# Tile counting of a graph layer: five units of 328 tiles, dealt out between the gathered groups

## The chip, the cores and the metric

The kernel runs on one core of one Trainium2 chip. The time is the device time of one execution in microseconds, here 2799.81 us as the median of three runs.

## The reference

A node-feature table `x` (12,500 nodes by 256) goes through a layer norm, a graph layer, a second layer norm and a mixture of eight experts. The graph layer is what the change touches:

```python
def _L0_gnn_ref(node_feats, src, dst, eps, W1, b1, W2, b2, gamma, beta):
    neigh = jax.ops.segment_sum(node_feats[src], dst, num_segments=n)
    h = (1.0 + eps) * node_feats + neigh
    h = jax.nn.relu(h @ W1 + b1) @ W2 + b2
    mean = jnp.mean(h, axis=0)
    var = jnp.mean(jnp.square(h - mean), axis=0)
    h = (h - mean) * jax.lax.rsqrt(var + BN_EPS) * gamma + beta
```

There are 200,000 edges, sorted by destination: `dst = int(12500 * u**2)` for random `u`, so the first nodes have by far the most edges. The sources are random.

## The kernel before

The 200,000 edges are 1563 tiles of 128 edges, in the order of their destinations. `stage_edges` sums the source rows of every edge into the destination rows in two ways, and mixes both.

**Gathered groups.** A group is 8 tiles (GT). GpSimd issues one indirect DMA per tile (L744), which brings 128 source rows of the node table into a buffer; there are three buffers (RG), and three groups make an iteration. GpSimd may refill a buffer when TensorE has released it (`s_free`, at the end of `gathered`, L795). VectorE makes the one-hot matrices of the group's destinations (L1005 `e_rel`, L1010 `e_hot`), TensorE multiplies them with the gathered rows (L790, 16 matmuls), and VectorE adds the sums of the group before into the node blocks (L993, two instructions). A group whose destinations lie in two blocks does this once per block (a window). A register word per group says which blocks.

**Counted tiles.** The hottest 256 tiles (HT) are not gathered. VectorE makes two one-hot matrices of a tile (L1046 and L1048: source block by destination column, and source row), TensorE multiplies them into a tally in PSUM (L808), and VectorE adds the tally into the matrix `counts` (98 source blocks by 136 columns) at the column of the destination (L1063). Four tiles in a row share a tally at first, then two, then one (g in SEGMENTS), as long as they span at most five destinations (TW). When the tiles of a unit are counted, VectorE folds the last eight columns (L1098), TensorE multiplies `counts` with the whole node table, which SyncE brings in 25 pieces of 512 KB (L704, L830), VectorE adds the product to two node blocks (`spread`, L1075), and ScalarE clears `counts` for the next unit (L904, 13 instructions). There are three units (SEGMENTS), of 144, 64 and 48 tiles.

**The order.** Each engine runs its own program, and the order in each is fixed by the same list of iterations. `sections` walks over them: `build` iterations first count 24 or 16 tiles, in bodies of eight, and then handle the three gathered groups; four `mix` iterations (MIX) handle two pieces behind each group; `plain` iterations are groups alone, with a quad at the end of most.

**Quads.** A quad is 512 nodes, whose edges are all in. It goes through the two layers on TensorE (L840 transposes, L848, L854) and ScalarE (L912, L915, L920), and its statistics on VectorE (`measure`, L1085; the copy for the transposes is L1090). `AT` says behind which iteration a quad stands; quads 1 to 24 follow one another from iteration 27 on, quad 0 stands behind iteration 25, and the last quad behind everything.

A test on the edge list in `stage_norm` decides whether the counting fits the data; if not, a general and slow path takes all edges (`general_rounds`).

What a group waits for on VectorE and TensorE stands in these lines:

```python
                        dve.wait_ge(s_sum, turn)
                        dve.wait_ge(s_add, turn)
                        add_window(dve.snap(1 - place)).then_inc(s_add, 1)
```

## Time and profile before

| | |
|---|---|
| median of 3 runs | 2799.81 us (2795.89 to 2807.99) |
| profiled execution | 2807.59 us |
| its span | 2805.5 us |
| mean granted TensorE clock | 0.808 |
| TensorE matmuls busy | 1710.0 us (61%) |
| VectorE busy | 1451.2 us (52%) |
| ScalarE busy | 674.4 us (24%) |
| GpSimd busy | 1805.8 us (64%) |
| gathers (L744) | 1320, 955 ns on average |
| HBM read, written | 275.92 MB, 75.58 MB |

The span is measured from the first to the last instruction of the program, the execution's time lies 2.1 us above it. GpSimd is the busiest engine, but no engine is near 100%: the program has four stages with different limits (norms and table until about 130 us, edges until about 1957 us, routing until about 2190 us, experts until the end). The change is in the second stage. A busy share over the whole span says little about it; what counts is which engine sets its pace and what that engine waits for.

### The profile page before, as it was taken

How to read it: one execution, taken by the hardware profiler on the slowest of the kernel's cores; microseconds unless marked ns; L12 is line 12 of the kernel's file. 1: busy time of each engine (PE TensorE's matmuls, PEld its weight loads, DVE VectorE, ACT ScalarE, POOL GpSimd, SP SyncE). 2: the span in 40 equal slices, each digit the busy share in tenths (PEclk: the TensorE clock that was granted, in tenths of full speed). 3: DMA queues.
4: the chain of work that ended last, by engine and by line, in shares of the span. 5: the costliest groups of instructions: out<-in, count | busy, mean ns of one | idle time of the engine just before them, and what ended most of it. 6: DMA issues, size and time to landing. Idle time of an engine off the chain costs nothing. (4 is left out here: it accounts for less than half of the span.)

```text
span 2805.5 us, 39125 instructions
## 1 busy us (share of the span) xinstructions
PE 1710.0 (61%) x9059; PEld 1019.1 (36%) x9060; DVE 1451.2 (52%) x4196; ACT 674.4 (24%) x1061; POOL 1805.8 (64%) x1798
## 2 busy tenths in 40 slices
PE   0045555446445566777745665577664888979984
PEld 0012222113212233333323333344553555656663
DVE  8856642573265222323323322332786566858885
ACT  6610000000000001111100110012664654535543
POOL 0066667667757767777777777771355577857876
PEclk9986567567757678999968878798665899989997
DMA  7533357336725744433333333332663322140220
GB/s 237 194 96 106 99 168 235 103 108 200 227 86 156 230 143 121 128 113 105 105 106 106 106 106 105 105 104 38 202 215 127 99 79 81 33 141 24 86 92 15
DMA packets 201051, 345.76 MB, mean 123 GB/s; under 512 B 65494, under 2 KB 129324, under 8 KB 200871
## 3 DMA queue, kind: packets, MB, share of 16 engines
q0 software_dynamic: 74304, 195.51, 24.0%
q1 hardware_dynamic: 124422, 146.96, 16.4%
q8 instruction: 93, 1.52, 0.2%
q10 hardware_dynamic: 2144, 1.05, 0.1%
q14 instruction: 88, 0.71, 0.1%
HBM read 275.92 MB, written 75.58 MB: 125 GB/s over the span
## 5 line engine op out<-in xcount | busy, mean ns | idle before, releaser
L744 POOL DMA_INDIRECT e_got<-table,e_idx x1320 | 1260.6, 955 | 514.2 <-issue 383.5
L790 PE MATMUL e_sums<-e_got,e_hot 128*128 128x256 f16 x2720 | 463.1, 344 | 509.3 <-DMA e_got<-table,e_idx 341.6
L790 PEld LDWEIGHTS e_sums<-e_got,e_hot 128*128 x2720 | 316.7, 121 | 666.8 <-issue 580.1
L993 DVE SCALAR_TENSOR_TENSOR nodes<-e_sums,above,nodes x171 | 82.6, 483 | 705.8 <-PE e_sums L790 690.8
L1665 POOL TENSOR_TENSOR x_midl<-x_midf,x_midh 128x512 f16<-128x512 f32 x200 | 293.9, 1497 | 96.6 <-ACT x_midh L1784 92.3
L808 PE MATMUL e_tally<-w2f 128*128 128x490 f16 x256 | 124.4, 542 | 302.1 <-DVE w2f L1048 298.8
L1010 DVE TENSOR_SCALAR e_hot<-ring,e_rel x1360 | 249.1, 275 | 65.2 <-DVE e_rel L1005 59.5
L1741 PE MATMUL x_down<-x_w2h,x_midh 128*128 128x256 f16 x736 | 203.9, 277 | 14.3 <-DVE x_yb L1884 12.5
L912 ACT ACTIVATE e_hT<-e_up 128x1024 f32<-128x1024 f32 (+1 forms) x25 | 25.2, 1006 | 746.6 <-PE e_up L840 746.6
L1741 PE MATMUL x_down<-x_w2l,x_midh 128*128 128x256 f16 x736 | 204.0, 277 | 0.0
L1741 PE MATMUL x_down<-x_w2h,x_midl 128*128 128x256 f16 x736 | 203.8, 277 | 0.0
L1680 POOL DMA_INDIRECT out<-x_res,x_nodei x128 | 141.9, 1108 | 88.7 <-DVE x_res L1899 51.3
L848 PE MATMUL e_up<-e_hT,W1s 128*128 128x512 f32 (+1 forms) x400 | 179.1, 602 | 27.4 <-ACT e_hT L912 27.4
L854 PE MATMUL e_up<-e_mid,W2s 128*128 128x512 f32 (+1 forms) x400 | 174.9, 590 | 19.2 <-ACT e_mid L915 19.2
L808 PEld LDWEIGHTS e_tally<-w2f 128*128 128x128 f16 x256 | 26.3, 103 | 397.3 <-issue 396.9
L904 ACT ACTIVATE counts<-e_zero 128x536 f32<-128x536 f32 (+1 forms) x39 | 20.6, 615 | 611.8 <-PE e_product L830 611.8
L1270 POOL DMA_INDIRECT slot_rows<-r_row,r_slots x100 | 97.5, 975 | 98.3 <-DVE r_slots L1496 74.5
L1717 PE MATMUL x_up<-x_xTh,x_w1h 128*128 128x512 f16 (+1 forms) x400 | 148.7, 372 | 3.2 <-ACT x_midh L1784 3.2
L1717 PE MATMUL x_up<-x_xTl,x_w1h 128*128 128x512 f16 (+1 forms) x400 | 148.1, 370 | 0.0
L1717 PE MATMUL x_up<-x_xTh,x_w1l 128*128 128x512 f16 (+1 forms) x400 | 148.1, 370 | 0.0
L1784 ACT ACTIVATE x_midf<-x_up,x_b1s 128x512 f32<-128x512 f32 x200 | 138.6, 693 | 23.8 <-PE x_up L1717 13.8
L1784 ACT ACTIVATE x_midh<-x_up,x_b1s 128x512 f16<-128x512 f32 x200 | 137.5, 688 | 0.0
(209 smaller groups left out, 2681.9 us busy)
## 6 DMA issues: line engine op xcount, KB each, us to landing
w1f<-table SPq DMA_DIRECT2D x72, 512.0 KB, 4.5
e_got<-table,e_idx POOLq DMA_INDIRECT x1320
slot_rows<-e_zero SPq DMA_DIRECT2D x64, 268.0 KB, 2.7
x_row<-slot_rows SPq DMA_DIRECT2D x32, 536.0 KB, 7.3
table<-n_pair SPq DMA_DIRECT2D x25, 512.0 KB, 3.0
counts<-in_x SPq DMA_DIRECT2D x24, 512.0 KB, 5.0
r_xin<-in_x SPq DMA_DIRECT2D x24, 512.0 KB, 5.0
out<-r_row SPq DMA_DIRECT2D x24, 512.0 KB, 3.3
```

The source lines that it names most:

```text
L744: pool.indirect_dma_start(got[:, r, t, :], None, table.rearrange("p h d -> (p h) d"), bass.IndirectOffsetOnAxis(ap=idx[:, r, t:t + 1], axi ...
L790: ins = nc.tensor.matmul(sums[:, place, 0:D], hot[:, place, t, :], got[:, r, t, half * D:(half + 1) * D], start=(t == 0 and half == 0), st ...
L808: nc.tensor.matmul(tally[:, i // g % 2, 0:KEY], tall[:, i % OR, KEY:OH], tall[:, i % OR, 0:KEY], start=(i % g == 0), stop=(i % g == g - 1) ...
L848: ins = nc.tensor.matmul(up[:, c % 2, 0:width], W1s[:, j, c * P:(c + 1) * P], hT[:, j, 0:width], start=(j == 0), stop=(j == DK - 1))
L854: ins = nc.tensor.matmul(up[:, c, 0:width], W2s[:, j, c * P:(c + 1) * P], mid[:, j, 0:width], start=(j == 0), stop=(j == H1C - 1))
L1010: ins = nc.vector.tensor_scalar(hot[:, place, t, :], plan.ring[:, ring_at(shift)], rel[:, place, t:t + 1], None, ALU.is_equal)
L1270: pool.indirect_dma_start(buf, bass.IndirectOffsetOnAxis(ap=slots[:, j, t:t + 1], axis=0), row[:, j, t, :], None, bounds_check=bound, oob_ ...
L1665: nc.gpsimd.tensor_tensor(midl[:, j % 2, c, :], midf[:, c % MB, :], midh[:, j % 2, c, :], ALU.subtract).then_inc(s_mlo, 1)
L1680: pool.indirect_dma_start(out, bass.IndirectOffsetOnAxis(ap=nodei[:, j, t:t + 1], axis=0), res[:, r, t, :], None, bounds_check=bound, oob_ ...
L1717: ins = nc.tensor.matmul(up[:, c % MB, 0:tiles * P], w[:, h, k, cols], x[:, j % 2, k, 0:tiles * P], start=(n == 0), stop=(n == len(passes) ...
L1741: ins = nc.tensor.matmul(down[:, t, :], m[:, j % 2, k, rows], w[:, h, k, :], start=(n == 0), stop=(n == len(passes) - 1))
L1784: ins = nc.scalar.activation(m, up[:, c % MB, :], ACT.Relu, bias=b1s[:, h, c:c + 1], scale=MID_SCALE / (X_SCALE * W_SCALE))
```

## The change

The tiles to be counted are now 328, in five units of 144, 64, 48, 40 and 32 tiles. `UNIT_TILES` lists how many tiles an iteration has: 24 in the first four, 16 in the next three, 8 in all others that count. They are dealt out over the three groups of the iteration (`tiles_at`): 24 as 8, 8, 8; 16 as 5, 5, 6; 8 as 2, 3, 3, each share ahead of its group. Tiles up to 96 share a tally by four, up to 168 by two, the rest have one each. The gathered groups are 155 instead of 165 (NG), in 52 iterations instead of 55.

VectorE adds a group's tally one group late: after the one-hots of the next tile, also across a gathered group (`counted`); before, each body of eight ended with the last tally's add. The column of each add is loaded by itself; before, one load brought the columns of a body.

Units and quads now overlap: `AT` gives every quad an iteration and a place in it, from iteration 10 on. Eleven quads stand in iterations that count tiles, nine in mixed ones, and four in the last two iterations, where quads 0, 22, 1 and 23 stand at (50, 0), (50, 2), (51, 0) and (51, 2). `spread` stands in the iteration behind the last piece, and ScalarE's clearing behind the quads of the last mixed iteration. All loops over iterations in this stage but GpSimd's are written out; so are the loops of SyncE in `stage_norm` and of GpSimd's scatter in routing. The constants:

```diff
-SEGMENTS = (((4, 24, 4), (2, 24, 2)), ((1, 16, 2), (3, 16, 1)), ((3, 16, 1),))
-NU = len(SEGMENTS)
-BODY = 8
+UNIT_TILES = ((24, 24, 24, 24, 16, 16, 16), (8,) * 8, (8,) * 6, (8,) * 5, (8,) * 4)
+GROUPS = ((96, 4), (168, 2), (328, 1))
+NU = len(UNIT_TILES)
...
-NIT = -(-(ET - HT) // (GT * RG))
-NG = NIT * RG
+NG = -(-(ET - HT) // GT)
+NIT = -(-NG // RG)
...
+SPREAD = {n + 1: u for n, (u, i) in MIXED.items() if i == MIX - 1}
+AT = {2: (10, 2), 3: (13, 2), 4: (16, 2), 5: (18, 2), 6: (22, 2), 7: (24, 2), 8: (26, 2), 9: (28, 2), 10: (31, 2),
+      11: (33, 2), 12: (34, 2), 13: (36, 2), 14: (38, 2), 15: (40, 2), 16: (41, 2), 17: (43, 2), 18: (44, 2),
+      19: (46, 2), 20: (47, 2), 21: (49, 2), 0: (50, 0), 22: (50, 2), 1: (51, 0), 23: (51, 2)}
...
+        def tiles_at(n, r):
+
+            tiles = TILES.get(n, ())
+            return tiles[len(tiles) * r // RG:len(tiles) * (r + 1) // RG]
```

On TensorE:

```diff
-                def build(u, start, n, first, tiles, g):
-
-                    if u > 0:
-                        pe.wait_ge(s_clear, u)
-                    with pe.Fori(start, start + n) as it:
-                        with pe.Fori(0, tiles // BODY):
-                            for i in range(BODY):
-                                pe.wait_ge(s_tall, tile)
-                                pe.reg_add(tile, tile, 1)
-                                nc.tensor.matmul(tally[:, i // g % 2, 0:KEY], tall[:, i % OR, KEY:OH], tall[:, i % OR, 0:KEY],
-                                                 start=(i % g == 0), stop=(i % g == g - 1)).then_inc(s_tile, 1)
-                        for r in range(RG):
-                            gathered(it, r)
...
+                for n in range(NIT):
                     for r in range(RG):
-                        gathered(n, r)
...
+                        for t in tiles_at(n, r):
+                            count(t)
+                        if n * RG + r < NG:
+                            gathered(n, r)
+                        for number in pieces_at(n, r):
+                            piece(number)
+                        for q in quads_at(n, r):
+                            quad(q)
                 quad(NQ - 1, LAST)
```

On ScalarE:

```diff
+                blank(0)
+                for n in range(NIT):
+                    if n in SPREAD and SPREAD[n] + 1 < NU:
+                        blank(SPREAD[n] + 1)
+                    for r in range(RG):
+                        for q in quads_at(n, r):
+                            quad(q)
```

On VectorE:

```diff
-                            for i in range(BODY):
-                                one_hots(i)
-                                if i % g == 0 and i > 0:
-                                    count(i // g - 1, g)
-                            count(BODY // g - 1, 0)
...
+                def count(group):
+
+                    last_tile = len(GROUP_OF) - 1 - GROUP_OF[::-1].index(group)
+                    column = dve.value_load(plan.cols[0:1, group:group + 1], min_val=0, max_val=P - 1)
+                    dve.wait_ge(s_tile, OR + last_tile + 1)
+                    if group > 0:
+                        dve.wait_ge(s_count, group)
...
+                def counted(t):
+
+                    one_hots(t)
+                    if t in FIRST:
+                        dve.wait_ge(s_blank, (FIRST.index(t) + 1) * COUNT_ZEROS)
+                    elif GROUP_OF[t - 1] != GROUP_OF[t]:
+                        count(GROUP_OF[t - 1])
...
+                        for t in tiles_at(n, r):
+                            counted(t)
+                        if n * RG + r < NG:
+                            gathered(n, r)
+                        if n in SPREAD and r == 0:
+                            spread(SPREAD[n])
+                        for q in quads_at(n, r):
+                            quad(q)
```

**TensorE, from the end of a quad to the next gathered group.** Before, in the loop of plain iterations (L848 and L854 are the quad's layers, L790 the group's matmuls; ISA rows work on registers):

```order
L854 MATMUL e_up<-e_mid,W2s 128x512 [waits e_mid_s]
L854 MATMUL e_up<-e_mid,W2s 128x512 x7
L873 REGISTER_ALU
L873 COMPARE_AND_BRANCH
L779 TENSOR_LOAD words
L779 ISA x2
L782 ISA [waits e_got0]
L783 UNCONDITIONAL_BRANCH
L787 ISA [waits e_add,e_hot_s]
```

Now, behind iteration 13:

```order
L831 MATMUL e_up<-e_mid,W2s 128x512 [waits e_mid_s]
L831 MATMUL e_up<-e_mid,W2s 128x512 x7
L796 MATMUL e_tally<-w2f 128x490 [waits e_tall_s] x2
L774 TENSOR_LOAD words
L774 ISA x2
L777 ISA [waits e_got0]
L778 UNCONDITIONAL_BRANCH
L782 ISA [waits e_add,e_hot_s]
```

Two tallies of the next iteration now stand between the quad and the group.

**VectorE, the tiles in front of a group's one-hots.** Before, one of the eight tiles of a body in a unit counted one by one (L1046 and L1048 make the one-hots, L1063 adds the tally before):

```order
L1053 ISA [waits e_tile]
L1046 TENSOR_SCALAR w2f<-iota,key 128x490
L1053 ISA
L1048 TENSOR_SCALAR w2f<-iota,low 128x128
L1050 ISA
L1060 ISA [waits e_count,e_tile]
L1063 TENSOR_TENSOR counts<-counts,e_tally 128x98x5
L1065 REGISTER_ALU
```

Now, from the copy of a quad's rows (L1027) to the first one-hots of the next iteration's first group:

```order
L1027 TENSOR_SCALAR e_hT<-nodes 128x1024
L975 TENSOR_SCALAR w2f<-iota,key 128x490 [waits e_tile]
L977 TENSOR_SCALAR w2f<-iota,low 128x128
L983 TENSOR_LOAD cols
L983 ISA x2
L988 ISA [waits e_count,e_tile]
L988 TENSOR_TENSOR counts<-counts,e_tally 128x98x5
...
L947 TENSOR_LOAD words
L947 ISA x2
L951 UNCONDITIONAL_BRANCH
L951 ISA
L953 REGISTER_ALU
L953 TENSOR_SCALAR e_rel<-cold,least,base 128x8
```

The six rows from L975 to L988 stand twice, where the line of dots is, and the group's `e_rel` and one-hots come behind the second add. Each add has a load of its own.

## Rows read from the trace of the kernel before

**Rows 1.** The line of the gather: durations (min, median, max) in ns, then idle time before it.

```profile
L744 POOL DMA_INDIRECT e_got<-table,e_idx x1320: 940/946/4984, 136.6 to 1904.5; - x189
...
  PEq L795: 123.9, 57
```

**Rows 2.** Timeline at the stage's end: start us, us, engine, line, names.

```profile
1904.52 0.95 POOL L744 DMA_INDIRECT e_got<-table,e_idx  x1 [0.30 <-issue]
...
1957.45 1.52 DVE L1372 BATCH_NORM_AGGREGATE r_bnv<-stats 128x2 f32<-128x150 f32 x2 [0.30 <-PEq L663]
```

**Rows 3.** Timelines of GpSimd and TensorE, 170 to 192 us, first counting iterations.

```profile
169.94 1.04 POOL L744 DMA_INDIRECT e_got<-table,e_idx  x1 [0.30 <-issue]
180.25 0.94 POOL L744 DMA_INDIRECT e_got<-table,e_idx  x1 [9.27 <-PEq L795]
...
175.71 3.59 PE L790 MATMUL e_sums<-e_got,e_hot 128*128 128x256 f16 x16 [4.02 <-DVE e_hot L1010]
...
186.34 1.92 PE L790 MATMUL e_sums<-e_got,e_hot 128*128 128x256 f16 x16 [1.72 <-DVE nodes L993]
189.14 0.99 PE L808 MATMUL e_tally<-w2f 128*128 128x490 f16 x4 [0.88 <-DVE w2f L1048]
```

**Rows 4.** Timelines of GpSimd, TensorE and ScalarE around quad 1, 1041 to 1090 us.

```profile
1042.44 0.95 POOL L744 DMA_INDIRECT e_got<-table,e_idx  x1 [0.30 <-issue]
...
1054.65 3.59 PE L790 MATMUL e_sums<-e_got,e_hot 128*128 128x256 f16 x16 [6.38 <-DMA e_got<-table,e_idx]
1064.95 3.59 PE L790 MATMUL e_sums<-e_got,e_hot 128*128 128x256 f16 x16 [6.70 <-DMA e_got<-table,e_idx]
...
1079.05 7.13 PE L854 MATMUL e_up<-e_mid,W2s 128*128 128x512 f32 x16 [0.78 <-ACT e_mid L915]
1086.02 1.91 PE L790 MATMUL e_sums<-e_got,e_hot 128*128 128x256 f16 x16
1089.64 1.92 PE L790 MATMUL e_sums<-e_got,e_hot 128*128 128x256 f16 x16 [1.71 <-DVE nodes L993]
...
1086.32 1.26 ACT L920 ACTIVATE nodes<-e_up,b2s 128x512 f32 x2 [7.32 <-PE e_up L854]
```

**Rows 5.** Windows: stretch, length, busy PE, PEld, DVE, ACT, POOL, granted clock, DMA share, GB/s.

```profile
150.00:390.00 240.00, 123.97 (x456) 52.19 (x456) 158.70 (x566) 0.55 (x2) 148.90 (x155) 0.68 0.35 106
390.00:500.00 110.00, 63.83 (x266) 32.20 (x266) 24.74 (x101) 0.00 (x0) 83.19 (x89) 0.72 0.68 224
1300.00:1400.00 100.00, 72.01 (x296) 39.73 (x296) 33.40 (x128) 15.11 (x21) 75.71 (x80) 0.93 0.37 105
```

**Rows 6.** Timelines of GpSimd and TensorE in mixed iteration 7, 397 to 424 us.

```profile
398.12 0.95 POOL L744 DMA_INDIRECT e_got<-table,e_idx  x1 [0.30 <-issue]
...
412.43 3.59 PE L790 MATMUL e_sums<-e_got,e_hot 128*128 128x256 f16 x16 [4.80 <-DMA e_got<-table,e_idx]
```

**Rows 7.** Timelines of VectorE: a tally's latency at 157 us, single tiles at 577 us.

```profile
157.51 0.67 DVE L1063 TENSOR_TENSOR counts<-counts,e_tally 128x490 f32 x1 [0.85 <-PE e_tally L808]
...
577.12 0.33 DVE L1046 TENSOR_SCALAR w2f<-iota,key 128x490 f16<-128x490 f16 x1
...
577.53 0.66 DVE L1063 TENSOR_TENSOR counts<-counts,e_tally 128x490 f32 x1
578.10 0.49 DVE L1046 TENSOR_SCALAR w2f<-iota,key 128x490 f16<-128x490 f16 x1
```

**Rows 8.** Timelines of VectorE: gathered groups at 560 us, a second window at 1885 us.

```profile
560.48 0.29 DVE L1005 TENSOR_SCALAR e_rel<-cold,least,base  x1 [0.72 <-issue]
561.12 1.43 DVE L1010 TENSOR_SCALAR e_hot<-ring,e_rel  x8 [0.35 <-DVE e_rel L1005]
...
564.65 0.29 DVE L1005 TENSOR_SCALAR e_rel<-cold,least,base  x1 [0.97 <-issue]
...
1885.18 0.30 DVE L1005 TENSOR_SCALAR e_rel<-cold,least,base 128x8 f32 x1 [0.29 <-issue]
```

**Rows 9.** Groups of instructions, 136 to 1906 us: the piece matmuls.

```profile
L830 PE MATMUL e_product<-w1f,counts 128*128 128x512 f16 x294 | 89.2, 452 | 19.5 <-DMA w1f<-table 14.4
```

**Rows 10.** Timeline of ScalarE, 490 to 520 us: the clearing of the counts.

```profile
500.15 6.87 ACT L904 ACTIVATE counts<-e_zero 128x536 f32<-128x536 f32 x13 [349.60 <-PE e_product L830]
```

More of the change, by code:

```diff
@@ L325, in _ @@
                     load(q, q, 0)
-                with sp.Fori(1, NQ // R5 - 1) as it:
+                for it in range(1, NQ // R5 - 1):
                     for j in range(R5):
@@ L813, in mix, with count @@
[L813 to L827 removed]
+                def count(t):
+                    group = GROUP_OF[t]
+                    pe.wait_ge(s_tall, t + 1)
+                    nc.tensor.matmul(tally[:, group % 2, 0:KEY], tall[:, t % OR, KEY:OH], tall[:, t % OR, 0:KEY],
+                                     start=(t == GROUP_OF.index(group)), stop=(group not in GROUP_OF[t + 1:])
+                                     ).then_inc(s_tile, 1)
@@ L832, in piece, with quad @@
                     ins.then_inc(s_used, 1)
-                def quad(k, width=QN):
-                    if not (isinstance(k, int) and k == 0):
+                def quad(q, width=QN):
+                    k = ORDER.index(q)
+                    if k > 0:
                         pe.wait_ge(s_h2, k * DK)
@@ L1129, in _, with quad @@
-                tile = counter(dve, "tile", 1)
-                counted = counter(dve, "counted", 1)
-                columns = [dve.alloc_register(f"column{i}") for i in range(BODY)]
-                dve.sem_inc(s_count, 1)
-                sections(build, mix, plain)
+                        nc.vector.bn_stats(stats[:, c, q * 6:q * 6 + 6], nodes[:, q, c * QN:c * QN + width])
+                def quad(q):
+                    k = ORDER.index(q)
+                    if k > 0:
+                        measure(ORDER[k - 1])
+                    nc.vector.tensor_scalar(hrow.rearrange("p t d -> p (t d)"), nodes[:, q, :], 1.0, None,
+                                            ALU.mult).then_inc(s_hrow, 1)
@@ L1274, in _ @@
                 pool.wait_ge(s_rows, 1)
-                walk(pool, [(scatter, 0)], NQ, R5)
+                for q in range(NQ):
+                    scatter(q, q % R5)
                 for j in range(R5):
```

303 lines of the change are left out of this document (94 added, 209 removed).

## The prediction

> **What bounds the kernel now.** I read four views in this order: the gather's own line, the timeline around its waits, the timeline of a counting iteration and of a quad, and the windows for the granted clock. The change lies in the stage that gathers edges, from the first gather at 136.6 us to the start of the next stage at 1957.5 us [rows 1, 2]. GpSimd issues its 1320 gathers. One takes 0.95 us and the next starts 1.25 us after it [rows 1, 3]: 1320 x 1.2515 = 1652 us of a stretch of 1904.5 + 1.0 - 136.6 = 1769 us. The missing 117 us are waits: 57 waits for TensorE's release (L795), 123.9 us with the usual 0.3 us in each [rows 1], 6.8 us for late index lists, and 4.0 us of one long first gather (4984 ns). So 112.5 us are real waits, 93% of the stretch is GpSimd's own pace, and only two things can shorten it: fewer gathers, or fewer waits. A group is 8 gathers, 10.0 us; an iteration three groups, 30.0 us.
>
> Where do the waits come from? From the iterations that count tiles. At 169.94 + 1.04 GpSimd stops; 24 tiles must be counted first, then TensorE multiplies the group at 175.71 for 3.59 us, and 0.95 us after its end GpSimd goes on, 9.27 us late [rows 3].
>
> **How late TensorE may be.** A group whose first gather started at 1042.44 is multiplied from 1054.65, 12.2 us later [rows 4]. Its buffer is wanted 3 x 10.0 us after that start, 0.95 us after the release [rows 3]. With 3.6 us of matmuls the slack is 30.0 - 0.95 - 12.2 - 3.6 = 13.3 us. A quad (the node blocks' two layers) sits between two groups on TensorE: matmuls of one group end at 1064.95 + 3.59 = 1068.54, those of the next at 1086.02 + 1.91 = 1087.93 [rows 4]. That is 19.4 us for one group, 9.4 over the pace, and below 13.3: in the old plain loop a quad costs nothing. This works because VectorE had the next one-hots ready while TensorE was in the quad.
>
> **Fewer gathers.** 165 groups become 155: 80 gathers x 1.2515 = **-100.2 us**, on the bounding engine. The 72 tiles that replace them cost no gather. The two new units read the table twice more (50 pieces of 512 KB); in the old mixed iterations the gathers kept their pace with the pieces beside them, and the DMA share was 0.68 [rows 5], so I book nothing for them. Their price is a later landing: a mixed group that began at 398.12 was multiplied from 412.43, after 14.3 us instead of 12.2 [rows 6, 4]. Between 0 and 2.1 us I take 1.3 off the slack there, nearer that row.
>
> **The old waits.** Tiles dealt out 8, 5 or 2 to 3 before each group no longer make 24 stand in a row: **-112.5 us** if nothing took their place.
>
> **What takes their place.** New is that 11 quads share iterations with tiles. The one-hots of a group now stand on VectorE behind the counts of its tiles, and with one tile per count each count waits for a tally that TensorE can make only after the quad. So from the end of a quad: tally and its latency 0.6 (0.85 from the end of the tile's one-hots, which are ready here [rows 7]), count 0.6 [rows 7], load of the group's word, `rel` and one-hots 0.97 + 0.29 + 0.35 + 1.43 = 3.0 [rows 8], 0.3 to the matmul, 1.9 us of it. Release to release: 17.6 + 6.4 = 24.0, and about 1 us because VectorE copies the quad's rows only after its adds: **15 us over the pace**, more than 13.3. Where the group after the quad has no tile it stays 10.3.
>
> How fast is that won back? A group costs VectorE 564.65 - 560.48 = 4.17 us [rows 8]; a tile with its count 578.10 - 577.12 = 0.98 us, some a little more, so 1.04 [rows 7]. With 2.67 tiles that is 6.95 us, and a load of the column in front of each count comes on top. That load isn't visible alone. Bounds: nothing (it runs behind the one-hots, 0.25 us of them), or the 0.68 us by which a group's first `rel` (0.97 us of idle) comes later than one without the load and two branches (0.29 us) [rows 8]; I take 0.25, nearer the lower end since one-hots run ahead of it. So 7.6 us with TensorE at its upper level (2.4 GHz). At its lower (1.2), the chain is 0.3 + 3.59 + 0.9 [rows 3] + 0.6 to the first count, 0.6 + 1.1 for the next, 3.0: 10.1 us. In the old counting iterations both matmul lengths stand side by side (3.59 and 1.92; see 1.92 right behind a quad [rows 3, 4]) at a granted clock of 0.68, while 1300 to 1400, with quads, had 0.93 [rows 5]. The middle is 8.8: **1.2 us won back per group**.
>
> The Trainium skill ("DMA: Bandwidth & Descriptors", Latency and other measured facts) puts the floor of a `tensor_load` at about 600 ns. The rows' 0.68 us, with two branches in it, agrees. If all 220 counts paid it openly it would be 132 us on VectorE, and the sum would be that of the slower rival below.
>
> A quad that finds the slack used up by the last one waits 15 less what the groups in between (its own excluded) won back. By iteration: 13: 0.6 (8 groups, whose tiles are partly counted in pairs, so 1.8 each); 16: 15 - 8 x 1.2 = 5.4; 18: 10.3 - 6 = 4.3; 24 and 26: 15 - 5 x 1.2 = 9 each; 28: 4.3; 33: 8.1 (the boundary behind 32, below, left 4.5 of slack); 34, right behind it: 15 - 2 x 1.2 = 12.6; 36: 9; 43: 9; 44: 12.6. Sum **+84**.
>
> **The unit boundaries.** Behind iterations 10, 22 and 41 a quad is followed by ScalarE's clearing of the counts: ten last piece matmuls at 0.30 [rows 9] make 3, quad 17.6, ScalarE's last copies end 1.4 later (1087.58 against 1086.18 [rows 4]), clearing 6.9 [rows 10], tile, count and one-hots 5.3, matmuls 3.6 = 38, or 28 over. Less 13.3, and 1.3 for the landing: 16 each, and 7 more at 41, where a quad at 40 had used up slack. Sum **+55**. Before, ScalarE's clearing was followed by a stall too, but of 24 or 16 tiles. Behind 32 there is no quad: 3 + 6.9 + 5.3 + 3.6 = 18.8, 8.8 over, no wait. **Unit 0** has no quads; 8 tiles in fours cost 4.17 + 8 x 0.41 + 2 x 0.82 = 9.1 us a group on VectorE, some 10.5 at the low level; 12 groups by 0.5: **+6**.
>
> **The end.** Iterations 46 to 51 hold 7 quads and the last short one. On TensorE: 7 x 17.6 + 17.6, 21 windows (a group's one-hots and matmuls run once per window; the last groups have two) x 3.62 (1089.64 - 1086.02 [rows 4]), 98 piece matmuls x 0.30 [rows 9] = 246, plus 12.2 to the first: 258, with a copy here and there 260 us. The old 17 last groups took 170 and another 52 from the last gather to the stage's end [rows 2], 222. **+38**. TensorE is what is late there, not the gathers.
>
> Unrolled loops in the first stage and in routing: nothing; GpSimd and SyncE wait for data there.
>
> **Sum.** -100.2 - 112.5 + 84 + 55 + 6 + 38 = **-30 us**. The profiled execution took 2807.6 us (span 2805.5), so 2778; against the median of the runs shown (2799.8) the same step gives **2770 us**.
>
> **Rivals.**
> 1. *Slower: nothing is won back in counting iterations.* Place: VectorE's count in front of a group's one-hots. It decides once a group with tiles takes 10 us or more, that is with TensorE at the lower level (10.1 us above) or loads in the open. Then the eleven quads cost about 145, boundaries 58, unit 0 20, the end 45: 268, against 212.7 gained: **+55, 2855 us**. For: 0.68 of granted clock where tiles were counted, and every matmul after a pause ran 3.59 us. Against: quads now lie between, and with quads it was 0.93. Chance 0.30.
> 2. *Faster: TensorE stays at the upper level and the load hides.* Won back 2.4 per group: quads 38, boundaries 47, end 38: 123. **-90, 2710 us**. Chance 0.15.
> 3. *The counting never holds up one-hots*, all waits go, only the end is dearer: -212.7 + 38 = **-175, 2625 us**. Against it: the order of the program, tallies behind the quad. Chance 0.03.
> 4. *The change doesn't do what it says*: the program tests the edge list and falls back to a slow general path if a count's tiles span more than 5 destinations, or a unit more than 128. From the reference's formula the widest group spans 5 exactly, the units 105 to 116; the last counted destination is 548 of 1024 allowed. It should hold. Otherwise hundreds of us slower. Chance 0.02.
>
> **How the numbers follow.** Forecast 0.50. Its own spread (load 0 to 0.68, 0.6 to 1.8 us won back) is -75 to +20. A measurement of this kernel can tell about 0.5% (14 us) from no change. Of the forecast's 0.50, 0.29 lie below -14, 0.17 within, 0.04 above; of rival 1's 0.30, 0.03 lie within. Faster: 0.29 + 0.15 + 0.03 = 0.47. Same: 0.20. Slower: 0.04 + 0.27 + 0.02 = 0.33. The range takes in rivals 1 and 2: 2705 to 2860; outside lie rivals 3 and 4 and the tails, under 0.2. The forecast's own range is 2725 to 2820.
>
> **What would show it.** 1240 gathers; GpSimd's waits for L774's release about 150 us, at iterations 11, 23 and 42 (14 to 22 us each), and after 24, 26, 33, 34, 36, 43 and 44 (9 to 13); hardly any in iterations 0 to 10. After a quad, the tally at once and the group's matmuls 4 to 5 us later instead of at once. A count's idle before it of 0 to 0.5 us. From the last gather to the next stage 70 to 80 us instead of 52. The forecast is wrong if groups with tiles that follow a quad come at more than 9.5 us (rival 1) or at under 8 (rival 2), or if the waits at 11, 23 and 42 are missing.

## The result: 7827 us, and the profile after

| | before | changed |
|---|---|---|
| median of the runs, us | 2798.5 (4 runs, 2795.9 to 2808.0) | 7826.8 (4 runs, 7819.4 to 7831.8) |
| ratio | | 2.795, 95% interval 2.788 to 2.802 |
| span of the profiled execution, us | 2805.5 | 7829.9 |
| granted clock, mean | | 0.934 |
| instructions recorded | | 65731 |

The forecast was 2770 us. The changed kernel takes 5028 us more than the old one, and no wait of a GpSimd-bound stage could be that large: the page has to be read for work that was not there before. Lines of the page of the changed kernel, its first line and four groups of instructions (columns: line, engine, operation, out<-in, count, busy and mean ns of one, idle before them and what ended it):

```profile
span 7829.9 us, 65731 instructions
...
L719 POOL DMA_INDIRECT e_got<-table,e_some x1568 | 1485.3, 947 | 3584.6 <-DMA e_some<-targets 3163.3
L760 PE MATMUL e_sums<-e_got,e_hot 128*128 128x256 f16 x3904 | 909.9, 413 | 4296.2 <-DMA e_got<-table,e_some 3957.8
...
L728 POOL DMA_INDIRECT e_got<-table,e_idx x1240 | 1179.5, 951 | 539.5 <-issue 366.4
...
L912 DVE SCALAR_TENSOR_TENSOR nodes<-e_sums,nodes 128x256 f32 x488 | 207.2, 425 | 3476.5 <-PE e_sums L760 3476.5
```

The line of the gather [rows 1] has become two. L728, with 1240 gathers of 951 ns, is what the prediction described. L719 is another place in the program: the general path, that handles all edges four tiles at a time with indices loaded into `e_some`. 1568 gathers are 392 rounds of 4, all edges of the list. GpSimd is idle for 3163 us of them, waiting for the next round's lists. The timeline of GpSimd in the changed kernel shows one round and the change-over (columns: start, length, engine, line, names, idle before):

```profile
136.52 4.32 POOL L719 DMA_INDIRECT e_got<-table,e_some  x1 [6.38 <-DMA e_some<-targets]
...
152.97 0.94 POOL L719 DMA_INDIRECT e_got<-table,e_some  x1 [8.37 <-DMA e_some<-targets]
154.22 0.95 POOL L719 DMA_INDIRECT e_got<-table,e_some  x1 [0.30 <-issue]
...
5199.12 0.95 POOL L719 DMA_INDIRECT e_got<-table,e_some  x1 [0.30 <-issue]
5207.57 0.95 POOL L728 DMA_INDIRECT e_got<-table,e_idx  x1 [7.50 <-PEq L768]
```

From 136.5 to 5207.6 us, 5071 us, the slow path runs, 12.9 us a round; nothing overlaps, since one round's lists, gathers, matmuls and adds follow each other. In the middle of that stretch VectorE starts one round's add at 2512.51, SyncE asks for the next lists at 2512.53, the gathers run from 2515.37 to 2520.06, the matmuls start at 2522.32 and the next add at 2524.44. Then the stage of the prediction runs as well, from 5207.6 to the next stage at 6990.3 us: 1783 us, where before it took 1821 [rows 2]. It adds nothing there: with `general` set the program gives it destinations and keys of -1, which match no row, and one window for every group (2480 matmuls at L785, 2560 in the repaired kernel below). So the 1783 us don't measure the change.

So the fourth rival had come about, "the change doesn't do what it says". The program itself decides: VectorE computes a list of conditions on the sorted destinations, and `general` is the number of rounds of the slow path, 0 if all hold. The list has six conditions (`wrong[0]` to `wrong[5]`), and the prediction had examined three: the span of a count, the width of a unit, the last counted destination. Two of the others ask for the order of the counted tiles; by the reference's formula both hold. The sixth is `wrong[3]`, fed by `BOUNDS` and `closed_before`:

```
return max([0] + [QN * (q + 1) for q, (it, _) in AT.items() if it <= group // RG])
...
then(nc.vector.tensor_tensor(wrong[3], block8[:, 0, :], bound, ALU.add))
```

A quad overwrites the rows of 512 nodes; from its iteration on, no group may still bring an edge to one of them. The table puts quad 5 (nodes 2560 to 3071) behind iteration 18. By the reference's formula the first group of iteration 18, group 54, starts at destination 2970, 102 too low. Every other quad of the table satisfies the condition, the closest quad 9 with 5 to spare (the old table's closest, quad 23, had 40). That was arithmetic; the runs had to show it.

### The profile page after: what moved, and what is told of

It is laid out like the page before. It is cut to its first block and busy times, and to the rows that moved or that the text cites. A ratio compares the mean times of both kernels' runs of the same rounds, so it can differ in the third digit from the quotient of the medians.

```text
span 7829.9 us, 65731 instructions
## 1 busy us (share of the span) xinstructions
PE 2688.4 (34%) x12991; PEld 1538.8 (20%) x12992; DVE 2252.5 (29%) x7571; ACT 688.4 (9%) x1087; POOL 3209.3 (41%) x3284
## 5 line engine op out<-in xcount | busy, mean ns | idle before, releaser
L719 POOL DMA_INDIRECT e_got<-table,e_some x1568 | 1485.3, 947 | 3584.6 <-DMA e_some<-targets 3163.3
L760 PE MATMUL e_sums<-e_got,e_hot 128*128 128x256 f16 x3904 | 909.9, 413 | 4296.2 <-DMA e_got<-table,e_some 3957.8
L760 PEld LDWEIGHTS e_sums<-e_got,e_hot 128*128 128x128 f16 x3904 | 501.8, 137 | 4703.6 <-issue 4515.4
L728 POOL DMA_INDIRECT e_got<-table,e_idx x1240 | 1179.5, 951 | 539.5 <-issue 366.4
L912 DVE SCALAR_TENSOR_TENSOR nodes<-e_sums,nodes 128x256 f32 x488 | 207.2, 425 | 3476.5 <-PE e_sums L760 3476.5
L785 PE MATMUL e_sums<-e_got,e_hot 128*128 128x256 f16 x2480 | 486.8, 380 | 402.9 <-DVE e_hot L958 243.5
L870 ACT ACTIVATE e_hT<-e_up 128x1024 f32<-128x1024 f32 (+1 forms) x25 | 25.2, 1007 | 6358.6 <-PE e_up L817 6312.9
L785 PEld LDWEIGHTS e_sums<-e_got,e_hot 128*128 x2480 | 318.6, 133 | 577.0 <-issue 467.2
L906 DVE TENSOR_SCALAR e_hot<-iota,e_rel 128x128 f16<-128x128 f16 x1952 | 376.7, 256 | 17.4
L920 DVE CAST e_somef<-e_some 128x4 f32<-128x4 int32 x392 | 66.6, 170 | 670.5 <-DMA e_some<-targets 664.3
L958 DVE TENSOR_SCALAR e_hot<-ring,e_rel x1240 | 229.6, 274 | 59.8 <-DVE e_rel L953 55.3
L988 DVE TENSOR_TENSOR counts<-counts,e_tally 128x490 f32 x220 | 146.4, 666 | 302.4 <-PE e_tally L796 270.3
L1649 PE MATMUL x_down<-x_w2h,x_midh 128*128 128x256 f16 x736 | 203.0, 276 | 14.5 <-DVE x_yb L1792 12.6
L975 DVE TENSOR_SCALAR w2f<-iota,key 128x490 f16<-128x490 f16 x328 | 120.6, 368 | 150.7 <-ACT counts L865 132.7
```

Source lines behind the costliest of these rows:

```text
L719: pool.indirect_dma_start(got[:, 0, t, :], None, table.rearrange("p h d -> (p h) d"), bass.IndirectOffsetOnAxis(ap=some[:, 0, t:t + 1], ax ...
L728: pool.indirect_dma_start(got[:, r, t, :], None, table.rearrange("p h d -> (p h) d"), bass.IndirectOffsetOnAxis(ap=idx[:, r, t:t + 1], axi ...
L760: ins = nc.tensor.matmul(sums[:, 0, 0:D], hot[:, 0, t, :], got[:, 0, t, half * D:(half + 1) * D], start=(t == 0 and half == 0), stop=(t == ...
L785: ins = nc.tensor.matmul(sums[:, place, 0:D], hot[:, place, t, :], got[:, r, t, half * D:(half + 1) * D], start=(t == 0 and half == 0), st ...
L906: ins = nc.vector.tensor_scalar(hot[:, place, t, :], plan.iota[:, 0:P], rel[:, place, t:t + 1], None, ALU.is_equal)
L912: return nc.vector.scalar_tensor_tensor(out=row, in0=sums[:, place, 0:D], scalar=1.0 / X_SCALE, in1=row, op0=ALU.mult, op1=ALU.add)
```

## The experiments

Ratios are to the kernel before, run beside the new one on the same chip.

**1. One number: quad 5 one iteration later.**

```
-AT = {2: (10, 2), 3: (13, 2), 4: (16, 2), 5: (18, 2), ...
+AT = {2: (10, 2), 3: (13, 2), 4: (16, 2), 5: (19, 2), ...
```

> One number differs from the changed kernel: quad 5 (nodes 2560 to 3071) stands behind iteration 19 instead of 18. Theory A, found after the result: the changed kernel's own list, not its work, fails the test that a quad may only close once all groups with its edges are past (group 54, the first of iteration 18, starts at destination 2970, 102 below 3072), and so the 392 rounds of the slow path ran. Then here the 1568 gathers of that path are gone, 1240 are left, and the time falls by about 5000 us, to 2770 us by the sum of the prediction (2710 to 2855 with its neighbours), with waits of 14 to 22 us at iterations 11, 23 and 42. Rival B: another condition fails too (spans of a count, a unit's width). Then the slow path still runs and the time stays at 7827 us. Rival C: the new order is slow by itself, and the slow path is only part of the 5000 us: over 3000 us remain.

Measured: 2773.9 us (4 runs, 2771.1 to 2782.0), ratio 0.988 (0.986 to 0.991). The slow path is gone, 5053 us with it. Theory A of the expectation holds; its rivals B (another condition fails too) and C (the new order is slow by itself) fall. The forecast for a kernel that does what it says was 2770.

**2. The slow path forced in the kernel before.** The condition for quad 23 made stricter by 64.

```
-    return max([0] + [QN * (q + 1) for q, it in AT.items() if it <= group // RG])
+    return max([0] + [QN * (q + 1) + (64 if q == NQ - 2 else 0) for q, it in AT.items() if it <= group // RG])
```

> The kernel before, with the condition for quad 23 made stricter by 64 destinations, which its list does not meet (its margin there is 40); nothing else is changed, and its order of work is the old one. Theory A (the slow path is an addition of its own, whatever order follows): 392 rounds of 13 us come in front, about +5050 us, so 7850 us, 24 to 25 us off the changed kernel's 7827 plus or minus what the new order is worth by itself. Rival C (part of the 5000 us belongs to the new order): clearly less, under 7000 us.

Measured: 7932.4 us (2 runs), ratio 2.827. Groups of instructions of GpSimd in that run:

```profile
L732 POOL DMA_INDIRECT e_got<-table,e_some x1576 | 1501.3, 953 | 3652.2 <-DMA e_some<-targets 3220.4 <-issue 431.9
L744 POOL DMA_INDIRECT e_got<-table,e_idx x1320 | 1257.4, 953 | 499.9 <-issue 384.8 <-PEq L795 107.2 <-PEq L773 7.5
```

394 rounds cost 5127 us over the 2805.6 of the kernel before, 13.0 us a round, against 12.9 in the changed kernel. The slow path costs the same in either; the new order is not slow. The expected 7850 took 5050 us for 392 rounds, 12.9 each; two more rounds and 0.1 us each make up most of the difference. An order that leaves quad 5 at 18 and drops the test was not tried: it would read the quad's rows before the last edges are added to them.

From here on the repaired kernel is what the prediction's sum is held against, and the other runs change one thing in it.

**3. Tiles counted behind their group instead of ahead.** In the loops of TensorE and VectorE the loop over `tiles_at(n, r)` stands behind `gathered(n, r)`.

> As the first run, but the tiles dealt to a group are counted behind it instead of ahead of it, on TensorE and on VectorE. By the prediction's step on quads: the next group's one-hots are then ready during a quad, so a quad costs 19.4 us from group to group again instead of 24 to 25, and the +84 us for eleven quads among tiles falls to about 0 to 20; the boundaries stay. So 60 to 80 us below the first run of this call, about 2695 us. Rival: the order behind or ahead does not matter, since the next group's one-hots wait for its tally anyway once the list is filled: within 10 us of the first run.

Measured: 2762.6 us, ratio 0.984 (0.982 to 0.987), 11 us under the repaired kernel (intervals overlap), not 60 to 80. That is the rival's picture, 1 us outside its 10. TensorE and then VectorE in this run, around the quad behind iteration 24:

```profile
958.98 1.91 PE L785 MATMUL e_sums<-e_got,e_hot 128*128 128x256 f16 x16
...
964.95 2.61 PE L785 MATMUL e_sums<-e_got,e_hot 128*128 128x256 f16 x16 [3.34 <-DVE e_hot L958]
...
961.54 0.74 DVE L988 TENSOR_TENSOR counts<-counts,e_tally 128x490 f32 x1 [16.90 <-PE e_tally L796]
```

The group behind the quad is multiplied at once, as expected. But VectorE stands 16.9 us before the next count, whose tally comes behind the quad, and with it the one-hots of the second group. The wait is moved by one group, not removed: GpSimd waits 9.7 and 8.1 us for the quads of iterations 24 and 26, against 9.4 and 8.5.

**4. Dealing undone.** All tiles of an iteration ahead of its first group.

```
-            return tiles[len(tiles) * r // RG:len(tiles) * (r + 1) // RG]
+            return tiles if r == 0 else ()
```

> As the first run, but the tiles of an iteration are all counted before its first group, not dealt out over its three. By the prediction: in unit 0 that brings back 24 tiles in a row, 24 x 0.6 = 14 us of TensorE's and VectorE's time in one place, and so some 4 to 9 us of wait in most of the 4 first iterations and less after: +30 to +60 us. In the other units 8 tiles in a row are 8 x 1.04 to 1.3 = 8 to 10 us once per 30 us, won back by the two groups without tiles: about 0 there, and where a quad follows the third group it may even gain, since no count stands between the quad and ... the next iteration's first group has all eight: +5 us more for those. In sum 20 to 80 us over the first run. Rival: dealing out is worth nothing: within 10 us.

Measured: 2804.5 us (10 runs), ratio 0.999 (0.997 to 1.002): 30 us over the repaired kernel, in the expected range, for another reason. GpSimd in this run, in unit 0 and behind the quad of iteration 10:

```profile
172.94 0.94 POOL L728 DMA_INDIRECT e_got<-table,e_idx  x1 [2.96 <-PEq L790]
...
529.52 0.94 POOL L728 DMA_INDIRECT e_got<-table,e_idx  x1 [24.66 <-PEq L790]
```

In unit 0, where I had put most of it, there is one wait of 3.0 us. The cost is behind the three boundaries (24.7, 21.4 and 25.6 us at iterations 12, 24 and 43 instead of 16.3, 19.1 and 15.0) and behind the first two quads among tiles (9.4 and 9.3 at 15 and 18 instead of 2.3 and 5.2), 32 us in all. At a boundary all eight tiles now stand between the clearing and the first group's one-hots. Behind the other quads among tiles the wait is shorter or the same (7.7 instead of 13.6 us at 46), which takes some 10 us off again. So dealing is worth most at the boundaries, not in unit 0. The profiled execution (2793.7 us) lies 12 us over the repaired kernel's, so its waits account for that, not for all of the 30 us between the medians.

**5. Each count's column loaded twice.**

```
+                    dve.value_load(plan.cols[0:1, group:group + 1], min_val=0, max_val=P - 1)
                     column = dve.value_load(plan.cols[0:1, group:group + 1], min_val=0, max_val=P - 1)
```

> The repaired kernel (quad 5 behind iteration 19), with the column of each count loaded twice on VectorE instead of once; nothing else. It measures the load of the prediction by itself: 220 loads more, 2.67 per group of the iterations with tiles. The prediction booked 0.25 us for one, the slower rival 0.68 (in the open, two branches included). Win-back is what pays for quads there, so with 0.25 us a group takes 0.67 us longer: about 5 groups between quads, eleven quads, +35 us and some 5 us at the boundaries, +40 us in all. With 0.68 us: a group takes 1.8 us longer, nothing is won back and quads' waits pile up: +90 to +110 us. If loads hide (rival 2): within 10 us.

Measured: 2802.6 us (10 runs), ratio 1.000 (0.998 to 1.001), 0.011 over the repaired kernel's ratio: 31 us for 220 loads, 0.14 us each. VectorE in this run:

```profile
977.27 0.67 DVE L989 TENSOR_TENSOR counts<-counts,e_tally 128x490 f32 x1 [1.01 <-issue]
```

The same count in the repaired kernel has 0.38 us of idle (at 972.58, below), so one load in the open is 0.63 us. Over all 220 counts VectorE's idle time just before the add grows less, from 302 to 336 us, 0.15 us each, which fits the 31 us. In front of adds that wait for a tally it even falls, from 270 to 250 us: there the load passes while VectorE would have stood anyway. The Trainium skill ("DMA: Bandwidth & Descriptors", Latency and other measured facts) gives about 600 ns for a `tensor_load`. The 0.63 us agrees with that. The 31 us are near the 40 us that follow from the 0.25 us of the sum, and far from the 90 to 110 of the rival's open loads.

**6. Counts added two groups of tiles late.** A third tally buffer, and each count one step later.

```
-        tally = psum("e_tally", [P, 2, 2 * D], F32)
+        tally = psum("e_tally", [P, 3, 2 * D], F32)
...
-                    elif GROUP_OF[t - 1] != GROUP_OF[t]:
-                        count(GROUP_OF[t - 1])
+                    elif GROUP_OF[t - 1] != GROUP_OF[t] and GROUP_OF[t] - 2 >= GROUP_OF[max(f for f in FIRST if f <= t)]:
+                        count(GROUP_OF[t] - 2)
```

(`group % 2` becomes `group % 3`, and `fold` adds the last two.)

> The repaired kernel, with counts added two groups of tiles late instead of one (three tally buffers in PSUM instead of two). It takes away the wait of each count for a tally that TensorE can make only behind the group's matmuls or behind a quad. By the prediction's step on quads: the count in front of a group's one-hots then needs only tallies made before the quad, so a quad costs 19.4 us from group to group (9.4 over the pace, under the slack of 13.3) instead of 24 to 25, and a group with tiles takes 7.4 us (8.64 in the repaired kernel's trace at 971.70, less the wait of 1.24 for the tally). Nearly all of the +84 for quads goes, the boundaries (51 us there) stay: 65 to 80 us below the repaired kernel, 2695 to 2710 us. Rival: VectorE's own work (7.4 us and more at the lower clock) or ScalarE's copies set the pace of these groups, not the tally: less than 25 us.

Measured: 2711.2 us (4 runs), ratio 0.967 (0.965 to 0.969): 0.022 under the repaired kernel, 61 us; expected were 65 to 80. TensorE in this run, from the end of the same quad:

```profile
951.16 1.91 PE L785 MATMUL e_sums<-e_got,e_hot 128*128 128x256 f16 x16
...
957.52 3.36 PE L785 MATMUL e_sums<-e_got,e_hot 128*128 128x256 f16 x16 [3.52 <-DVE e_hot L958]
...
965.03 3.59 PE L785 MATMUL e_sums<-e_got,e_hot 128*128 128x256 f16 x16 [3.22 <-DVE e_hot L958]
...
971.19 3.36 PE L785 MATMUL e_sums<-e_got,e_hot 128*128 128x256 f16 x16 [1.44 <-DVE e_hot L958]
...
978.69 3.59 PE L785 MATMUL e_sums<-e_got,e_hot 128*128 128x256 f16 x16 [3.09 <-DVE e_hot L958]
```

From 957.52 three groups take 21.2 us, 7.1 each; in the repaired kernel one takes 8.6 (971.01 to 979.64, below), with matmuls as long as these. The waits of 9.4 and 8.5 us for the quads of 24 and 26 are gone. It was the tally's wait that set the pace of these groups. Waits of 7.5, 4.1 and 4.2 us stay at iterations 35, 36 and 46, behind the quads that stand closest together.

**7. In addition, the boundary quads one iteration later.** Quad 2 to 11, 6 to 23, 16 to 42, and 7, 8, 9, 18 by one.

> As the run with counts two groups late, and in addition the three quads that were followed by ScalarE's clearing stand one iteration later (2 from 10 to 11, 6 from 22 to 23, 16 from 41 to 42; 7, 8, 9 and 18 one later too, so that quads don't crowd). By the prediction's step on boundaries: a boundary is then 3 + 6.9 + 5.3 + 3.6 = 18.8 us, 8.8 over the pace and under the slack, as at iteration 32 of the changed kernel, where no wait is; the quad one iteration later finds it partly won back. The 16 to 19 us waits at the three boundaries (51 us) fall to 0 to 7 each: 35 to 50 us below the run with late counts alone. Rival: the clearing on ScalarE is not what they wait for but the last piece matmuls or their transfers: then the waits stay.

Measured: 2674.0 us (4 runs), ratio 0.955 (0.952 to 0.957), 37 us under run 6 on the same chip. TensorE, then ScalarE, at the first boundary:

```profile
483.80 0.37 PE L796 MATMUL e_tally<-w2f 128*128 128x490 f16 x1
...
510.55 1.07 PE L817 MATMUL e_up<-ident,e_hT 128*128 128x128 f32 x8
...
484.00 6.87 ACT L865 ACTIVATE counts<-e_zero 128x536 f32<-128x536 f32 x13 [334.54 <-PE e_product L806]
```

ScalarE clears straight behind the last piece matmuls, the quad comes 27 us later, and GpSimd does not wait at all from 470 to 535 us. Behind the other two boundaries waits of 4.3 us (iteration 25) and 7.2 and 5.2 us (44, 45) stay. The idle time of GpSimd before L728, for TensorE's release, in three kernels: 168.6 us in the repaired one, 107.8 in run 6, and here

```profile
L728 POOL DMA_INDIRECT e_got<-table,e_idx x1240: 940/946/4495, 135.9 to 1751.5; - x178
its engine sat idle before it (us, times) until:
  issue: 365.9, 1189
  PEq L790: 61.8, 43
```

This is faster than both kernels of the case, by 4.5% than the one before.

**8. Counts at once, and four units: on slower chips.** Two more kernels: one adds each count behind its own tile's one-hots in the repaired kernel; the other is run 7 without the fifth unit (296 tiles, 1272 gathers, quads placed anew by the same rule, and one iteration more at the end that holds a quad and no group).

```
-                    elif GROUP_OF[t - 1] != GROUP_OF[t]:
-                        count(GROUP_OF[t - 1])
+                    if GROUP_OF[t] not in GROUP_OF[t + 1:]:
+                        count(GROUP_OF[t])
```

```
-UNIT_TILES = ((24, 24, 24, 24, 16, 16, 16), (8,) * 8, (8,) * 6, (8,) * 5, (8,) * 4)
+UNIT_TILES = ((24, 24, 24, 24, 16, 16, 16), (8,) * 8, (8,) * 6, (8,) * 5)
```

> The repaired kernel (quad 5 behind iteration 19), with each count added at once, behind the one-hots of its own tiles, instead of one group of tiles later. It undoes that part of the change alone. Each count of one tile then waits in the open for its own tally, 0.9 us from the one-hots to the tally and 0.4 us for it, where in the repaired kernel only one count in a group waits, 1.2 us. By the prediction's model a group with tiles comes to some 11 us at the lower clock, over the pace of 10.0, so nothing is won back in the 16 iterations of units 1 to 4 that count single tiles, and the slower rival's picture appears: +60 to +130 us. Rival: the wait that bounds these groups is elsewhere (ScalarE, the landing), then within 20 us.

> As the fastest run so far (counts two groups late, boundary quads moved), but without the fifth unit: 296 tiles in four units, 1272 gathers instead of 1240, the quads placed anew by the same rule, the quads of nodes 0 to 1023 behind iterations 45 and 48 instead of 50 and 51. It measures what the last unit is worth. Gathers: +32 x 1.2515 = +40 us. Against it the end: in that run TensorE, not GpSimd, is late in the last iterations (26 us of waits in iterations 48 to 51, 78 us from the last gather to TensorE's end, 52 in the kernel before), and 12 us of waits at iterations 43 to 45. If the end is TensorE's as the prediction has it, these give back 20 + 22 + 12 = 54 us: 2660 us, 2645 to 2690. Rival: the end costs what it costs whatever the gathers do; then +30 to +40 us, 2705 to 2715.

Measured: 3338.4 us, ratio 0.951 (0.947 to 0.955), and 3254.6 us, ratio 0.927 (0.924 to 0.931). But the kernel before took 3503 us on this chip, so neither can be set beside the runs above. They were repeated with the kernel of run 7:

> The fastest kernel so far once more (counts two groups late, boundary quads moved), as the common measure for the two runs beside it: 0.9545 of the kernel before, within 0.004, on a chip where the kernel before takes about 2800 us. In the call before this one the kernel before took 3503 us on its chip, so those two ratios can't be set beside the earlier ones.

> Counts added at once, again, on a chip where the kernel before takes about 2800 us: by the prediction's model +60 to +130 us over the repaired kernel (2774), so 0.010 to 0.035 over the kernel before in ratio; within 20 us of the repaired kernel if something else bounds these groups. On the slower chip it was 0.9512 of the kernel before.

> Four units instead of five, again: 2660 us (2645 to 2690), that is 5 to 30 us below the first run of this call, if the end is TensorE's; +30 to +40 us over it if the fifth unit saves its 32 gathers in full.

The next chip was of the same kind (kernel before 3503.0 us): 3226.1 us, ratio 0.921 (0.915 to 0.926); 3338.6 us, 0.952 (0.948 to 0.956); 3255.5 us, 0.928 (0.922 to 0.934). And a third time, with the repaired kernel beside them:

> The repaired kernel again, as the measure for the two beside it. On a chip where the kernel before takes 2800 us: 0.988 of it within 0.003, as in the first call. On one where it takes 3500 us: between counts at once (0.951) and counts two late with moved quads (0.921), about 0.94.

> Counts added at once. On a chip of 2800 us: +60 to +130 us over the repaired kernel beside it, by the wait for its own tally before every count of a single tile (about 2.2 us per group more). On one of 3500 us, where the landing of a group's gathers holds each group up by 2.5 us and so VectorE has time to spare: less, +15 to +50 us. Rival: the tally's wait is not in the path: within 10 us on either.

> Four units, 1272 gathers, counts two late, quads placed anew. On a chip of 2800 us: 2660 us (2645 to 2690), 0.950 of the kernel before and not over its 0.9545 with five units, if the saved 40 us of gathers are given back at the end by TensorE; 0.965 to 0.970 if they are not. On one of 3500 us: 0.928 again, over the 0.921 of five units, since four groups more cost 4 x 12.3 us there.

Again a chip of that kind (kernel before 3545.5 us): repaired 3366.1 us, ratio 0.949 (0.947 to 0.952); counts at once 3385.6, 0.956 (0.953 to 0.958); four units 3272.4, 0.923 (0.919 to 0.927). So there, counting one group late is worth 19 us, within the 15 to 50 expected; what it is worth on a chip of 2800 us was not measured. Leaving out the fifth unit gained nothing there: 29 us slower beside run 7's kernel, with intervals that overlap. Since the quads moved too, the 29 us aren't the unit's alone, and whether it pays on the other chips stays open.

## Why the prediction was wrong, and what of it was right

**The step that failed** is the fourth rival's: "From the reference's formula the widest group spans 5 exactly, the units 105 to 116; the last counted destination is 548 of 1024 allowed. It should hold." Each number there is right, and the list is short by three of six conditions, one of which fails. It leaves out the places of the quads, whose inputs this change rewrote in full. 24 places stood in a new table; the old one had been built by rules. Checking it needed one destination per quad, the same arithmetic as for the spans. With it the slow path would have been the forecast; at 0.02 it was left out of the range. The runs showed 5053 us in its place: so much went when quad 5 moved by one iteration. The size, "hundreds of us", was wrong too. The larger part of it was in the rows: 392 rounds, each with three gathers by 1.25 us [rows 1, 3] and then 3.4 us from the last gather's start to the matmuls (12.2 less 7 x 1.25 [rows 4]), 7.2 us in a row, 2800 us by themselves. The matmuls, the add and the next lists' load, which no row of the kernel before prices, make it 12.9.

**The sum** for a kernel that does what it says was -30 us. The repaired kernel differs from it by one place in the table. Its median is 2773.9 us against 2770, its profiled span 2780.3 against 2775.5. Its gather line, its waits and the next stage's first instruction:

```profile
L728 POOL DMA_INDIRECT e_got<-table,e_idx x1240: 940/947/4477, 136.4 to 1859.0; - x178
...
  issue: 366.2, 1185
  PEq L790: 168.6, 43
...
L1280 DVE BATCH_NORM_AGGREGATE r_bnv<-stats x2: 772/802/832, 1937.7 to 1938.5; 128x2 f32<-128x150 f32 x2
```

Term by term:

| term | predicted | repaired kernel |
|---|---|---|
| fewer gathers | -100.2 | -100.1: 80 fewer at 1.2515 us again (the prediction has 0.1 too much) |
| old waits | -112.5 | gone: GpSimd first waits for TensorE at iteration 12 |
| eleven quads among tiles | +84 | +80: ten are left with quad 5 at 19, each with a wait, 83.2 us in all with 0.3 us in each |
| boundaries | +55 | +49: 16.3, 19.1 and 15.0 us, less 0.3 each |
| unit 0 | +6 | +2 over seven iterations, none of it a wait |
| end | +38 | +53: 275 us from the first gather of iteration 46 to the next stage, against 222 |

The terms of the last column sum to -28; the spans differ by 25.2, the medians on one chip by 31.7. That the total is within 5 us of the forecast is partly luck: the end cost 15 us more, the quads, boundaries and unit 0 together 14 us less.

**The quad among tiles.** VectorE in the repaired kernel, from the end of the quad behind iteration 24:

```profile
967.60 0.75 DVE L988 TENSOR_TENSOR counts<-counts,e_tally 128x490 f32 x1 [17.99 <-PE e_tally L796]
968.59 0.29 DVE L953 TENSOR_SCALAR e_rel<-cold,least,base 128x8 f32 x1 [0.25 <-issue]
969.25 1.44 DVE L958 TENSOR_SCALAR e_hot<-ring,e_rel  x8 [0.36 <-DVE e_rel L953]
...
972.58 0.67 DVE L988 TENSOR_TENSOR counts<-counts,e_tally 128x490 f32 x1 [0.38 <-issue]
...
974.90 0.74 DVE L988 TENSOR_TENSOR counts<-counts,e_tally 128x490 f32 x1 [1.24 <-PE e_tally L796]
...
977.23 0.29 DVE L953 TENSOR_SCALAR e_rel<-cold,least,base 128x8 f32 x1 [0.29 <-issue]
...
984.09 0.67 DVE L988 TENSOR_TENSOR counts<-counts,e_tally 128x490 f32 x1 [1.66 <-PE e_tally L796]
...
985.98 0.29 DVE L953 TENSOR_SCALAR e_rel<-cold,least,base 128x8 f32 x1
```

and TensorE beside it, with GpSimd's wait that follows:

```profile
967.09 0.58 PE L796 MATMUL e_tally<-w2f 128*128 128x490 f16 x2
971.01 3.04 PE L785 MATMUL e_sums<-e_got,e_hot 128*128 128x256 f16 x16 [3.34 <-DVE e_hot L958]
...
979.64 3.59 PE L785 MATMUL e_sums<-e_got,e_hot 128*128 128x256 f16 x16 [3.02 <-DVE e_hot L958]
...
988.46 3.59 PE L785 MATMUL e_sums<-e_got,e_hot 128*128 128x256 f16 x16 [2.62 <-DVE e_hot L958]
...
974.96 0.95 POOL L728 DMA_INDIRECT e_got<-table,e_idx  x1 [9.35 <-PEq L790]
```

Tally at once, group 3.9 us behind it (4 to 5 predicted), the next 8.6 us later (8.8 predicted as the middle, 1.2 won back). Rival 1 needed 10 us, rival 2 7.6. Run 6, where the tally's wait is gone, has 7.1.

That 8.8 came out is luck. It was the middle between 7.6 us at TensorE's upper level and 10.1 at its lower. But these groups ran at the lower level: their matmuls take 3.59 us, and the granted clock from 967 to 1012 us was 0.66. So the 10.1 us were the ones that applied, and the chain behind them was too dear. From 979.64 on it is 3.59 us of matmuls, 0.86 to the first count (0.9 + 0.6 predicted), 1.89 to the group's `rel` (0.6 + 1.1), and 2.48 to the next matmuls (3.0 + 0.3): 8.8 us. Two mistakes, in the clock and in the chain, cancelled. Rival 1 had one of its two conditions, TensorE at the lower level, and did not come about.

A wait that a quad causes shows two iterations later on GpSimd; predicted after 24, 26, 34, 36, 43, 44: 9, 9, 12.6, 9, 9, 12.6; measured 9.4, 8.5, 10.5, 8.6, 8.3, 13.6. After 33 it was 13.9 instead of 8.1, for which I have no cause. The 4.3 us predicted at 18 never came, with quad 5 at 19 in its stead.

**The boundary**, behind iteration 10: TensorE, ScalarE, VectorE, and GpSimd's wait.

```profile
494.96 7.13 PE L831 MATMUL e_up<-e_mid,W2s 128*128 128x512 f32 x16 [0.78 <-ACT e_mid L873]
...
513.95 3.59 PE L785 MATMUL e_sums<-e_got,e_hot 128*128 128x256 f16 x16 [2.62 <-DVE e_hot L958]
...
503.29 6.86 ACT L865 ACTIVATE counts<-e_zero 128x536 f32<-128x536 f32 x13
...
510.18 0.35 DVE L975 TENSOR_SCALAR w2f<-iota,key 128x490 f16<-128x490 f16 x1 [37.74 <-ACT counts L865]
...
518.47 0.94 POOL L728 DMA_INDIRECT e_got<-table,e_idx  x1 [16.27 <-PEq L790]
```

The chain is as worked out: quad, copies, 6.9 us of clearing, one-hots, matmuls. Run 7 took the quad out of it, and 37 us went. The waits show at the first gathers of iterations 12, 24 and 43, one later than the prediction's 11, 23 and 42. The 7 us more at 41 did not come: 15.0.

**The end** was mis-sized by 15 us. I had let TensorE start iteration 46 level with the gathers, 12.2 us behind the first one at 1662.36. But the quad of 44 hands it over late, and it starts 19.0 us behind:

```profile
1681.39 3.43 PE L785 MATMUL e_sums<-e_got,e_hot 128*128 128x256 f16 x16 [2.72 <-DVE e_hot L958]
```

That is 7 us. From there to the next stage it takes 256 us where the sum had 246 and some 2 for copies. In this stretch TensorE waits 13.4 us for pieces of the table and 10.1 us for gathered rows, for which the sum had no term; no run takes these waits apart. From the last gather to the next stage it is 77.7 us, 70 to 80 predicted. What lateness a stretch inherits belongs in its sum.

## What to carry to other kernels

A kernel that tests its input and has a slow path is first of all those tests: list every condition, and for each one that the change's tables or sizes feed, work out its margin, before any sum over engines. A margin of 5 destinations, as quad 9 has now, is part of the result. In the profile, a gather line split over two source lines says at once that another path ran. And where an engine counts for a later engine's benefit, ask how late the count may be: one more PSUM buffer was worth 61 us here, and taking the quads from directly ahead of ScalarE's clearing another 37.

## What was not expected of the hardware

On three of the five chips of the experiments the same programs took a quarter longer (kernel before 3503, 3503 and 3546 us; 2803 to 2806 on the two others), at a granted clock of 0.75 instead of 0.81 for the repaired kernel. The gather itself is as quick (953 ns on average, 956 on the first chip), yet the last one is issued 562 us later, so nearly all of the 587 us more in the profiled span lie in the stage of the edges. The repaired kernel on such a chip, GpSimd's line, then TensorE and GpSimd in unit 0:

```profile
L728 POOL DMA_INDIRECT e_got<-table,e_idx x1240 | 1182.3, 953 | 1109.0 <-PEq L790 647.4 <-issue 361.2 <-DMA e_idx<-rows_of 100.4
...
205.34 3.59 PE L785 MATMUL e_sums<-e_got,e_hot 128*128 128x256 f16 x16 [1.68 <-DVE e_hot L958]
211.80 2.20 PE L796 MATMUL e_tally<-w2f 128*128 128x490 f16 x5 [2.87 <-remote]
...
212.57 1.00 POOL L728 DMA_INDIRECT e_got<-table,e_idx  x1 [2.56 <-PEq L790]
```

The same place on the first chip, TensorE in the repaired kernel:

```profile
204.81 3.59 PE L785 MATMUL e_sums<-e_got,e_hot 128*128 128x256 f16 x16 [1.88 <-DVE e_hot L958]
208.55 2.12 PE L796 MATMUL e_tally<-w2f 128*128 128x490 f16 x5
```

Between a group's matmuls and what stands behind them on TensorE there are 2.9 us instead of 0.15, and GpSimd waits 2.6 us for its release, where on the first chip it does not wait. The expectations of run 8 put this down to a later landing of the gathers; these rows don't show that, the delay stands behind the matmuls. In unit 0 nearly every group waits so and takes 12.4 us instead of 10.0. Later groups are slower still (14.7 us on average over all 155), and there TensorE also waits 329.5 us in front of the piece matmuls for something that the profile names only `remote`, a releaser that it does not name on the first chip. The cause of both is open. On the chip of these rows the repaired change is worth more: 5.1% instead of 1.2%.
